# W1's two halves on two queues, chunk 5's right fields loaded instead of picked, and one chunk's product moved up, in a three-layer CIN kernel

## The reference

```python
X0 = inputs.reshape(-1, 32, 64)
Xi = X0
for W, b in ((W1, b1), (W2, b2), (W3, b3)):
    Wr = W.reshape(128, 32, Xi.shape[1])
    Xi = jnp.einsum('bhd,bmd,ohm->bod', X0, Xi, Wr) + b[None, :, None]
    pools.append(Xi.sum(axis=-1))
return concatenate(pools) @ fc_W.T + fc_b
```

## Time and profile before

| | |
|---|---|
| runs | 81.09, 81.17, 81.17 us; median 81.17 us |
| profiled execution, its own time | 81.42 us |
| its span, first to last instruction | 79.6 us |
| TensorE busy | 73.1 us, 92% of the span |
| GpSimd, VectorE, ScalarE busy | 48.7, 45.9, 34.9 us |
| data moved | 12.01 MB in 7529 packets |

### The profile page before, as it was taken

The page is one execution under the profiler, slowest core; times in us unless marked ns, Lnnn a source line. Parts: engine busy times, 40 slices in busy tenths (PEclk is TensorE's granted clock), DMA queues, the critical chain, the costliest instruction groups (busy, mean ns, idle before and its releaser), DMA issues.

```text
span 79.6 us, 1146 instructions
## 1 busy us (share of the span) xinstructions
PE 73.1 (92%) x372; PEld 52.3 (66%) x372; DVE 45.9 (58%) x45; ACT 34.9 (44%) x51; POOL 48.7 (61%) x48
## 2 busy tenths in 40 slices
PE   4999499978994999999999999999999999999970
PEld 1345176843440677888888888888888888886840
DVE  1067699786959999790649969992003003203541
ACT  1833997649955859975645520570300300000000
POOL 4999844999992693929166989619946004162400
DMA  0898999999985361714999700000000000000000
GB/s 26 243 366 280 355 377 350 382 389 384 376 288 138 96 175 44 215 34 94 404 381 315 301 8 0 4 0 0 0 0 0 0 0 0 8 0 0 0 0 0
DMA packets 7529, 12.01 MB, mean 151 GB/s; under 512 B 835, under 2 KB 3971, under 8 KB 7267
## 3 DMA queue, kind: packets, MB, share of 16 engines
q1 hardware_dynamic: 6915, 11.16, 41.0%
q10 hardware_dynamic: 608, 0.77, 3.1%
HBM read 10.88 MB, written 1.05 MB: 150 GB/s over the span
## 4 chain that ended last, share of the span: by engine, by line
PE 70%; DMA 10%; POOL 5%; DVE 4%; SPq 4%; issue 4%; ACT 1%; DVEq 0%; POOLq 0%
PE a_ps L586 28%; PE x_ps L586 25%; DMA x_in<-xl 10%; PE z_ps L580 4%; DVE r_in L475 3%; POOL feat L267 3%; PE a_ps L641 2%; PE a_ps L679 2%; PE a_ps L640 2%; PE x_ps L614 2%; SPq L196 2%; POOL xs L260 2%; PE x_ps L758 1%; SPq L184 1%; SPq L210 1%
## 5 line engine op out<-in xcount | busy, mean ns | idle before, releaser
L267 POOL TENSOR_TENSOR feat<-r_in,feat 128x1024 fp32r<-128x1024 f32 x8 | 19.5, 2442 | 6.3 <-ACT feat L358 5.9
L586 PE MATMUL x_ps<-feat,w_hi 128*128 128x512 f32 x64 | 19.2, 395 | 0.0
L586 PE MATMUL a_ps<-feat,a_hi 128*128 128x512 f32 x64 | 16.2, 395 | 0.0
L508 DVE SCALAR_TENSOR_TENSOR x<-a_ps,vec,x 128x512 f32<-128x512 f32 x7 | 5.2, 748 | 16.7 <-PE a_ps L641 16.6
L274 POOL TENSOR_TENSOR x<-x 128x512 f32<-128x512 f32 x6 | 7.8, 1293 | 10.9 <-DVE x L508 10.7
L586 PEld LDWEIGHTS x_ps<-feat,w_hi 128*128 128x128 f32 x64 | 11.9, 189 | 3.4 <-issue 0.8
L586 PEld LDWEIGHTS a_ps<-feat,a_hi 128*128 128x128 f32 x64 | 11.9, 188 | 2.7
L260 POOL TENSOR_TENSOR xs<-x_in,xs 32x512 fp32r<-32x512 f32 x7 | 9.8, 1395 | 5.7 <-ACT xs L358 5.4
L358 ACT ACTIVATE feat<-z_ps 128x1024 fp32r<-128x1024 f32 x8 | 8.2, 1026 | 6.5 <-DVE z_ps L475 6.5
L482 DVE TENSOR_TENSOR feat<-z_ps,feat 128x1024 fp32r<-128x1024 f32 x8 | 9.7, 1219 | 1.5 <-ACT feat L358 1.5
L358 ACT ACTIVATE feat<-r_in 128x1024 fp32r<-128x1024 f32 x8 | 8.5, 1058 | 3.0 <-DVE r_in L475 2.9
(11 more groups left out here) (76 smaller groups left out, 73.4 us busy)
## 6 DMA issues: line engine op xcount, KB each, us to landing
w_sb<-w SPq DMA_DIRECT2D x9, 512.0 KB, 8.7
x_in<-xl SPq DMA_DIRECT2D x8, 256.0 KB, 7.3
r_in<-xr SPq DMA_DIRECT2D x2, 1024.0 KB, 7.0
a_by_fields<-at_sb SPq DMA_DIRECT2D x8, 96.0 KB, 2.0
x<-x ACTq DMA_DIRECT2D x1, 512.0 KB, 4.6
x<-x SPq DMA_DIRECT2D x1, 512.0 KB, 5.9
w_sb<-w SPq DMA_DIRECT2D x1, 256.0 KB, 10.2
a_by_fields<-at_sb SPq DMA_DIRECT2D x4, 64.0 KB, 1.8
```

Of the source, the lines that this page charges most:

```text
L267: nc.gpsimd.tensor_tensor(feat[:, c, 1, of_half(1), :], z_of(c, 1), feat[:, c, 0, of_half(1), :].bitcast(f32), ALU.subtract).then_inc(lo_d ...
L508: nc.vector.scalar_tensor_tensor(out=x1[:, c, :], in0=a_ps[:, c % 2, :], scalar=vec[:, 3:4], in1=x1[:, c, :], op0=ALU.add, op1=ALU.mult).t ...
L586: nc.tensor.matmul(bank, weights[:, k, :], feat[:, c, part, k, :], start=(start and k == 0), stop=False)
```

## The change

It makes these edits. (1) W1's main tiles go from the second place of SyncE's list to the head of ScalarE's, ahead of `x16` and `vec`. (2) SyncE then loads x of chunk 1, W1's remainder tiles (before behind all of W2), x of chunks 2 and 3, and W3 behind these. (3) PICKED goes from 6 to 5: chunk 5's right fields are loaded, behind x of chunk 5, and its four picks fall away; chunks 6 and 7 swap their buffers of `r_in`, and chunk 6's load waits for chunk 5's `hi` and for GpSimd's `lo(5)`. (4) TensorE's list has chunk 1's and part of chunk 2's product further ahead, between the parts of v and the rounds, and rounds 2 and 3 behind them; `x1_product(5)` stands ahead of `a_product(0)`, and `a_product(4)` ahead of `x1_product(7)`. (5) The lists of ScalarE and VectorE follow: `rest_sum` comes right behind VectorE's `lo(0)` and `rest_lo` between chunk 2's two `mult`s; ScalarE saves x1 of chunks 0 to 5 earlier in its list, with x1 of chunk 2 behind the loads of `f2`; `product`s are put between the `mult`s of chunks 6 and 7.

```diff
--- before.py
+++ after.py
@@ -25,7 +25,7 @@
-PICKED = 6
+PICKED = 5
 X_BUFS = 4
...
@@ -165,13 +165,17 @@
+        def right_buf(c):
+
+            return (c - PICKED) % 2
+
         def z_of(c, half):
...
                 return r_in[:, 1, of_half(c % 2), :]
-            return r_in[:, c % 2, of_half(1), :]
+            return r_in[:, right_buf(c), of_half(1), :]
...
@@ -184,12 +188,12 @@
             def load_right(c):
-                if c % 2 == 0:
+                if c == PICKED:
                     sp.wait_ge(spread_done, 3)
                 else:
-                    sp.wait_ge(hi_done, count(PICKED - 1, 1))
-                    sp.wait_ge(lo_done[1], PICKED)
-                sp.dma_start(r_in[:, c % 2, :, :], xr[c]).then_inc(r_here[c % 2], 16)
+                    sp.wait_ge(hi_done, count(c - 1 if c == PICKED + 1 else c - 2, 1))
+                    sp.wait_ge(lo_done[1], c if c == PICKED + 1 else c - 1)
+                sp.dma_start(r_in[:, right_buf(c), :, :], xr[c]).then_inc(r_here[right_buf(c)], 16)
...
@@ -207,21 +211,21 @@
             load_x(0)
-            sp.dma_start(w1_sb[:, :, 0:TILES, :], w1[:, :, 0:TILES, :]).then_inc(w1_in, 16)
             load_x(1)
+            sp.dma_start(w1_sb[:, :, EVEN:, :], w1[:, :, EVEN:, :]).then_inc(w1_rest_in, 16)
+            load_x(2)
+            load_x(3)
             load_w3(0)
             load_w3(1)
-            load_x(2)
             load_w3(2)
             load_w3(3)
-            load_x(3)
             load_w2(0)
...
             load_w2(3)
-            sp.dma_start(w1_sb[:, :, EVEN:, :], w1[:, :, EVEN:, :]).then_inc(w1_rest_in, 16)
             load_x(5)
+            load_right(PICKED)
             load_x(6)
...
@@ -239,12 +243,12 @@
                 scratch.tensor, FC2_COL * EXT * M, [[0, 3], [M, H], [1, M]])).then_inc(f_rest_in, 16)
-            load_right(PICKED)
+            load_right(PICKED + 1)
             sp.wait_ge(lo16_done, 1)
...
             load_x(7)
-            load_right(PICKED + 1)
+            load_right(PICKED + 2)
             sp.dma_start(fcb_sb[:, :], fc_b).then_inc(fcb_in, 16)
...
@@ -380,6 +384,7 @@
+            act.dma_start(w1_sb[:, :, 0:TILES, :], w1[:, :, 0:TILES, :]).then_inc(w1_in, 16)
             act.dma_start(x16[:, :, :], bass.AP(x.tensor, 0, [[N, P], [HALF * COLS, 2], [1, N]])).then_inc(x16_in, 16)
...
@@ -389,68 +394,68 @@
             split_x(1)
+            hi(0, 0)
             act.wait_ge(w_sum, 1)
             copy(w1_hi[:, 0:TILES, :], w1_sb[:, 0, 0:TILES, :]).then_inc(w_hi_done, 1)
-            hi(0, 0)
             hi(0, 1)
+            split_x(2)
             save_zz(0)
-            split_x(2)
+            act.wait_ge(w_rest_sum, 1)
+            copy(w1_hi[:, EVEN:, :], w1_sb[:, 0, EVEN:, :]).then_inc(w_hi_done, 1)
             hi(1, 0)
+            split_x(3)
             hi(1, 1)
-            split_x(3)
             act.wait_ge(vt_ready, 1)
             copy(vt_sb[:, :], vt_ps).then_inc(vt_saved, 1)
+            hi(2, 0)
             act.wait_ge(v_ready, 1)
...
             copy(v_st[:, H + 8:H + 15], v_by_field[:, 1, 0:7]).then_inc(v_saved, 1)
-            hi(2, 0)
+            act.wait_ge(vec_in, 16)
+            save_x1(0)
+            hi(2, 1)
             split_x(4)
-            hi(2, 1)
             save_a(0)
...
             hi(3, 0)
-            act.wait_ge(w_rest_sum, 1)
-            copy(w1_hi[:, EVEN:, :], w1_sb[:, 0, EVEN:, :]).then_inc(w_hi_done, 1)
-            split_x(5)
+            save_x1(1)
             save_a(2)
             save_a(3)
+            split_x(5)
             hi(3, 1)
             hi(4, 0)
-            act.wait_ge(vec_in, 16)
-            save_x1(0)
+            save_zz(1)
             hi(4, 1)
-            save_x1(1)
-            save_zz(1)
             act.wait_ge(zeros_done, ZEROS)
...
                     scratch.tensor, (TILES * j + k) * M, [[(EXT + 1) * M, H], [1, (TILES - k) * M]])).then_inc(f_main_in, 16)
+            save_x1(2)
             hi(5, 0)
...
                 [P, H, 4])).then_inc(v_saved, 1)
-            save_x1(2)
+            save_x1(3)
             act.wait_ge(f_sum, 1)
             copy(a_hi[:, 0:TILES, :], f1[:, 0:TILES, :]).then_inc(a_hi_done, 1)
-            save_x1(3)
             act.wait_ge(f_sum, 2)
...
             copy(q_sb[:, :], q_ps).then_inc(q_saved, 1)
+            save_x1(5)
             hi(6, 0)
...
             hi(7, 1)
-            save_x1(5)
             save_x1(6)
...
@@ -466,8 +471,8 @@
                 else:
-                    dve.wait_ge(r_here[c % 2], 16)
-                    right = r_in[:, c % 2, tiles, :]
+                    dve.wait_ge(r_here[right_buf(c)], 16 * ((c - PICKED) // 2 + 1))
+                    right = r_in[:, right_buf(c), tiles, :]
                     if half == 0:
...
@@ -519,16 +524,16 @@
             lo(0)
+            rest_sum()
             dve.wait_ge(w_hi_done, 1)
...
             chunk(1)
-            chunk(2)
-            mult(3, 0)
-            rest_sum()
-            mult(3, 1)
-            lo(3)
+            mult(2, 0)
             dve.wait_ge(w_hi_done, 2)
             rest_lo(w1_sb[:, 0, :, :], w1_hi, w_lo_done)
+            mult(2, 1)
+            lo(2)
+            chunk(3)
             chunk(4)
...
@@ -542,11 +547,16 @@
             rest_lo(f1, a_hi, a_lo_done)
-            chunk(6)
+            mult(6, 0)
             product(0)
+            mult(6, 1)
             product(1)
-            chunk(7)
-            for c in range(2, CHUNKS - 1):
+            lo(6)
+            mult(7, 0)
+            mult(7, 1)
+            product(2)
+            lo(7)
+            for c in range(3, CHUNKS - 1):
                 product(c)
...
@@ -696,50 +706,55 @@
             v_part(1)
+            pick_right(2, 0)
+            x1_hi(1, 0)
             v_part(2)
-            pick_right(2, 0)
+            v_part(3)
             pick_right(2, 1)
-            v_part(3)
+            x1_lo(0, 1)
             pe.wait_ge(ident_done, 2)
...
             nc.tensor.transpose(v_ps, vt_sb[:, :], ident[:, :]).then_inc(v_ready, 1)
-            x1_lo(0, 1)
-            pick_right(3, 0)
+            x1_tail(0)
+            x1_lo(1, 0)
             a_round(0)
             a_round(1)
-            x1_hi(1, 0)
+            pick_right(3, 0)
+            x1_main(1, 1)
             pick_right(3, 1)
+            x1_low_weights(1, 1)
+            x1_lo(1, 1)
+            x1_tail(1)
+            x1_main(2, 0)
             a_round(2)
...
             pick_right(4, 0)
-            x1_lo(1, 0)
             pick_right(4, 1)
-            x1_hi(1, 1)
-            x1_lo(1, 1)
-            x1_tail(0)
-            x1_tail(1)
+            x1_low_weights(2, 0)
+            x1_lo(2, 0)
             spread16(1)
-            pick_right(5, 0)
-            x1_hi(2, 0)
-            x1_lo(2, 0)
-            pick_right(5, 1)
             x1_hi(2, 1)
             x1_lo(2, 1)
+            x1_hi(3, 0)
             x1_tail(2)
-            x1_product(3)
+            x1_lo(3, 0)
+            x1_hi(3, 1)
+            x1_lo(3, 1)
+            x1_tail(3)
             x1_product(4)
+            x1_product(5)
             pe.wait_ge(v_saved, 4)
...
             a_product(1)
-            x1_product(5)
             a_product(2)
...
             a_product(3)
+            a_product(4)
             x1_product(7)
-            for c in range(4, CHUNKS - 1):
+            for c in range(5, CHUNKS - 1):
                 a_product(c)
...
```

## The result

The changed kernel takes 85.48 us (84.52 to 86.35) against 81.17: 1.049 times as long, 95% interval 1.045 to 1.053. The prediction was 80.6, between 79.0 and 82.0. The profiled execution took 86.35 us, with a span of 84.5 against 79.6. It is the longest of the four executions, one of the slow runs, so its times behind 45 us are not those of a typical one.

A forecast was written before the change was run, and what follows sets the result against it. TensorE's work was taken to set the end once begun in earnest. Picks -0.9, their waits -0.5, TensorE's old point -0.55 and later waits +1.4 gave -0.55, 80.9 profiled; 80.6 against the median 81.17, range 79.0 to 82.0.

The forecast's parts named there:

- Part 2: The head: x16 lands at 7.3, vec at 7.5, so chunk 1's picks start at 12.5, 1.4 us late.
- Rival (b): Head: the two queues share the engines, x16 lands near 9, GpSimd's list starts 1.7 later: 82.3; chance 0.18.
- Part 3: GpSimd's idle 2.13 us before split_x(2) goes; lo(1) ends at 20.5 (20.60 before), so the head's loss is made good there.
- part 5: From x1_tail(0) at 20.75 through two rounds, TensorE reaches its old state of 25.96 at 25.4: -0.55 us.
- Parts 4 and 6: GpSimd's lo(1) holds VectorE's rest_lo until 20.75, x1_tail(0) waits; later waits at products 4 and 5, entered as 1.4 us.
- Part 7: Chunk 6's load, issued at 41.6, lands in 5.1 us; a_product(2) is covered by 0.8; cost between 0 and 1, taken as 0.
- rival (c): Chunk 6's load and x take 7 us instead of 5.1: 81.9 at worst, 81.3 in the middle; chance 0.15.
- rival (d): The head's gap of 2.4 us lowers TensorE's clock, some ten matmuls take twice 0.23: +2.3, 82.9; chance 0.05.
- part 1: Chunk 5's four picks dropped, -0.9 us; two waits before chunk 4's picks also go, -0.5.
- part 6: Chunk 5: product 4 waits 0.3, product 5 waits 1.3 for save_x1(3); sum between 0.3 and 1.7, taken as 1.4 us.

The follow-up runs named there:

- e3: The changed kernel with chunk 6's load of the right fields waiting for chunk 4's hi and lo instead of chunk 5's; 83.42 us, ratio 1.029.
- e5: The changed kernel with W1's main tiles back in the second place of SyncE's list, everything else left; 80.87 us, ratio 0.995.
- e7: The kernel before with W1's main tiles at the head of ScalarE's queue and nothing else; 84.85 us, ratio 1.046.
- e12: The changed kernel with SyncE holding its list behind x of chunk 1 until x16 has landed; 82.22 us, ratio 1.013.
- e6: The changed kernel with W1's main tiles back on SyncE's list and chunk 6's load waiting for chunk 4's readers; 80.34 us, ratio 0.991.
- e8: The changed kernel with 15 more matmuls on zeros filling the gap and chunk 6's load waiting for chunk 4's readers; 83.29 us.
- e2: The changed kernel with 21 instead of 6 matmuls on zeros behind the first picks; 84.00 us, ratio 1.033.
- e4: The changed kernel with the load of x for the sums ahead of chunk 6's right fields on SyncE's list; 83.74 us, ratio 1.034.
- e1: The changed kernel with x16 and vec ahead of W1's main tiles on ScalarE's queue; 85.92 us, ratio 1.048.

## Why the prediction was wrong, step by step

The forecast was 4.9 us too low. At the medians 1.7 of that is the head, which I had priced at 1.4 and which cost 3.1; 2.1 is chunk 6, priced at 0; and 1.1 is the base, the rest of the sum.

**Part 2 failed, and with it the sign.** `e3`, which has the head's loss and not chunk 6's, is slower than the kernel before; `e5`, with the head in time, is not. The part reasoned that 1.5 MB were in at 7.9 in whatever order and put `x16` at 7.3. But SyncE's list ran ahead at the same time: by 3.7 us it had issued W1's rest and x of chunks 2 and 3 as well, and the two queues then shared the engines. `x16` came at 8.6, `vec` at 9.2, GpSimd's list 1.35 later than my 7.9. Rival (b) had named this, with a landing near 9, for a chance of 0.18, and its price of 1.7 us is what the head cost beyond my 1.4; that the two agree so well is in part luck, as it has GpSimd's list 1.7 later and not 1.35. What I held against it, one packet of q1 beside q10 in half a microsecond, shows that q1 moved nothing then, and not why; `e5` and `e7` show the price, and `e12` that of the 8.6 the last 0.9 us are SyncE's backlog. The rule of the Trainium skill (DMA: Bandwidth & Descriptors, section Queues, rings and completion order) is that each engine switches between the queue rows it has work for packet by packet. The trace agrees in so far as both queues were served within one half microsecond (30 packets and 23, 58.8% and 25.0% of the engines' time); it doesn't show an even turn, as the window from 3.5 to 4.0 has 93 packets of q10 and 6 of q1.

**Part 3 failed in its comfort.** That GpSimd reaches `lo(1)`'s end where it did before is not what counts: TensorE's list was packed from the first picks on, so its start counts. From `e6` to `e3` `spread16(0)` moved from 9.56 to 12.27, 2.7 later, product 5 from 39.05 to 42.14, and the time by 3.1. Without the clock's fall (`e8`) they are 2.85, 2.95 and 2.95. A late head went through one to one. My sum did let the 1.4 us through, as part 5 counts from a `lo(1)` that ends at 20.5; what misled was to call that made good, for with the head in time `lo(1)` ends at 19.2 (`e6`).

**Parts 4 and 6 held.** The wait for `rest_lo` (0.9), the turn-taking at chunk 5 and the wait for `save_x1(3)` (0.9; mine 1.3) stand in the kernels with a timely head, at the operations named. In the changed kernel `rest_lo` was held too (1.17 us for 0.42), but TensorE came late enough not to wait.

**Part 7 was mis-sized.** The mechanism was right and the term for the landing was not: the cover of 0.8 us, worked out for a landing in 5.1, was enough before `a_product(2)` where the load took 4.8 or 4.9 (`e2`, `e4`), and in the profiled execution it took 6.9. That was rival (c), chance 0.15. It had the two waits one within the other, 1.3 at the worst; they came one behind the other, 1.25 and 0.92. At the medians they cost 2.1 us (`e3`).

**The clock of rival (d) fell and hardly mattered.** With the gap of 3.67 it went to 1.2 GHz, for which I had given 0.05 and 2.3 us. At the gap of 2.4 that the rival names it would hardly have: `e12`'s of 2.92 left it at 1.00. And 1.4 us of slower matmuls cost 0.13 in the end (`e8`).

**The base was too low as well.** With the head restored and chunk 6 early, `e6` takes 80.34. My parts, without the 1.4 us of the head, would give 79.2. The difference of 1.1 us is, as far as the rows show it:

- 0.3 at `x1_tail(0)`, which started at 19.67 where my sum without the head's 1.4 has 19.35;
- 0.25 from there through the two rounds and the matmuls around them to `x1_lo(1, 1)`: 4.24 us (19.67 to 23.91) for the 4.0 of part 5;
- 0.1 by a slip in part 5, as 24.7 + 1.9 - 1.1 is 25.5 and not 25.4;
- 0.2 in part 1, as chunk 4's picks still take 1.14 for 0.92;
- 0.25 between the profiled execution of the kernel before, in which I read all gaps, and its median;
- less 0.3 at product 5. Product 4 started at 35.00, and 13 matmuls (2.97) later product 5 could have started at 37.97; it started at 39.05. That is a wait of 1.1, where part 6 worked out 1.6 and entered 1.4. The 0.92 of the row is shorter, since it counts from the modelled end of the last matmul.

The remainder of about 0.3 I can't place.

The three rivals (b), (c) and (d) were priced as alternatives. They share a cause, a late head, or stand one behind the other, and they came together.

## What to carry to other kernels

A transfer moved to a second queue doesn't come for nothing: what stands behind it in that queue shares the engines with all that the first queue has issued by then. Before such a move, look for the smallest transfer behind it and who waits for it; here 3 KB of `vec` held GpSimd's whole list. (`x16` had landed only 0.6 us before it, so how much `vec` alone costs is not shown; the changed kernel with `vec` ahead of `x16` was not run.) And when an engine is packed from its first work on, ask what starts it, since slack further down no longer helps.

## What I had not expected of the hardware

TensorE's granted clock fell in or behind idle times of 3.6 to 5.0 us (`e3`, the changed kernel, `e7`, `e4`, `e1`) and stayed at 1.00 behind those of 1.0 to 2.9 us (`e5`, `e6`, `e12`). A 1 MB load, issued under like conditions, landed in 4.8 or 4.9 us in five kernels and in 6.9 in the profiled execution of the changed one. Where VectorE and GpSimd contended, the instruction that stood waiting went ahead of the other engine's next. At chunk 5 of `e6` that was GpSimd's `lo(4)`, and its two `lo`s took 5.77 us for 4.8. It went the other way as well: in the changed kernel VectorE's `main_lo`, issued at 13.93 behind a GpSimd `split_x`, took 1.76 us for 0.68 and ended at 15.69, and GpSimd's `lo(0)`, issued at 15.21, took 2.73 for 2.39.
